# Graph attention on one core: edge terms in three bf16 parts, and the attributes' share of the logits from 49 TensorE products

## The reference

```python
edge_emb = edge_attr_full @ ew.T + eb
xw = x @ W
xj = xw[src].reshape(-1, H, D) + edge_emb.reshape(-1, H, D)
xi = xw[dst].reshape(-1, H, D)
alpha = leaky_relu(einsum(xi, att_i) + einsum(xj, att_j))     # a logit per edge and head
amax = segment_max(alpha, dst); ea = exp(alpha - amax[dst])
alpha = ea / (segment_sum(ea, dst)[dst] + EPS)
aggr = segment_sum(xj * alpha[..., None], dst)
return aggr.mean(axis=1) + b
```

## Time and profile before

| | |
|---|---|
| median of 3 runs | 3387.27 us (3385.08 to 3389.48) |
| span of the profiled execution, which is its own time here | 3764.7 us |
| PE busy | 2439.0 us, 65% |
| DVE busy | 2004.0 us, 53% |
| POOL busy | 2210.5 us, 59% |
| ACT busy | 696.7 us, 19% |
| DMA, mean of the 16 engines | 195.78 MB, 52 GB/s over the span |
| first gather of layer 0 | at 475.50 us |

### The profile page before, as it was taken

The page is one execution under the profiler, slowest core; times in us unless marked ns, Lnnn a source line. Parts: engine busy times, 40 slices in busy tenths (PEclk is TensorE's granted clock), DMA queues, the critical chain, the costliest instruction groups (busy, mean ns, idle before and its releaser), DMA issues.

```text
span 3764.7 us, 48376 instructions
## 1 busy us (share of the span) xinstructions
PE 2439.0 (65%) x13595; PEld 2001.4 (53%) x13595; DVE 2004.0 (53%) x6216; ACT 696.7 (19%) x3102; POOL 2210.5 (59%) x2357
## 2 busy tenths in 40 slices
PE   6779726666582766658276665837576582766668
PEld 6679615555461655547165554725455461655546
DVE  8955624554472555547255554725454472555456
ACT  0078511111121111112111111211111121111112
POOL 0067466666626766662666666266676626666661
PEclk8555555555565555556555555655555565555556
DMA  3212122222202222221222222022222202222221
GB/s 101 97 60 80 30 52 54 53 52 57 49 24 51 54 51 53 56 49 30 47 54 52 53 56 49 25 53 54 50 53 57 50 24 50 54 50 53 52 49 40
DMA packets 114121, 195.78 MB, mean 52 GB/s; under 512 B 39897, under 2 KB 77272, under 8 KB 113864
## 3 DMA queue, kind: packets, MB, share of 16 engines
q0 software_dynamic: 62560, 130.25, 15.2%
q1 hardware_dynamic: 51304, 62.42, 5.3%
HBM read 180.86 MB, written 11.67 MB: 51 GB/s over the span
## 4 chain that ended last, share of the span: by engine, by line
DVE 36%; PE 25%; another core or an unknown queue 20%; issue 13%; DVEq 3%; POOL 1%; ACT 1%; ACTq 1%; DMA 0%; POOLq 0%
PE bank L745 10%; PE bank L747 6%; DVE acc L1200 4%; DVE into L1143 2%; DVEq L1016 2%; PE bank L718 2%; DVE pw L1161 2%; DVE alpha L1094 2%; PE bank L741 2%; PE bank L783 2%; DVE fwd L1150 2%; DVE lanes L1129 2%; DVE prod L1072 1%; PE bank L766 1%
## 5 line engine op out<-in xcount | busy, mean ns | idle before, releaser
L510 POOL DMA_INDIRECT ring<-table,srci x1955 | 1941.2, 993 | 937.6 <-issue 556.4
L745 PE MATMUL bank<-pw,ring 128*128 128x48 f32 x3910 | 1210.9, 404 | 203.3 <-issue 201.8
L745 PEld LDWEIGHTS bank<-pw,ring 128*128 128x128 f32 x3910 | 1014.9, 314 | 302.9 <-issue 231.1
L1200 DVE TENSOR_TENSOR acc<-acc,bank 128x288 f32 x490 | 222.8, 455 | 1128.7 <-remote 857.3
L747 PE MATMUL bank<-onehot,est 128*36 128x24 f32 x3910 | 632.6, 243 | 222.9 <-issue 221.7
L741 PE MATMUL bank<-zeros 128*128 128x288 bf16 x490 | 208.5, 426 | 697.1 <-DVE pw L1161 438.7
L747 PEld LDWEIGHTS bank<-onehot,est 128*36 128x36 f32 x3910 | 391.2, 149 | 393.9 <-issue 226.6
L741 PEld LDWEIGHTS bank<-zeros 128*128 128x128 bf16 x490 | 55.4, 113 | 752.0 <-DVE pw L1161 453.3
L586 ACT ACTIVATE dd<-dd 128x66 f32<-128x66 f32 x75 | 19.4, 258 | 2163.4 <-DVE dd L1154 1177.9
L580 ACT COPY ai_win<-ai_rows 128x48 f32 x1955 | 336.3, 229 | 432.6 <-issue 410.5
L491 POOL TENSOR_TENSOR ring<-ring,acc 128x512 f32<-128x512 f32 x98 | 117.1, 1195 | 250.1 <-ACT ring L545 246.7
(11 more groups left out here) (214 smaller groups left out, 2610.1 us busy)
## 6 DMA issues: line engine op xcount, KB each, us to landing
ring<-table,srci POOLq DMA_INDIRECT x1955
ai_rows<-lo_dram SPq DMA_DIRECT2D x28, 896.0 KB, 4.3
at<-in_attr SPq DMA_DIRECT2D x65, 224.0 KB
table<-ring SPq DMA_DIRECT2D x15, 390.0 KB, 3.5
table<-ring SPq DMA_DIRECT2D x5, 325.0 KB, 3.4
result<-ring SPq DMA_DIRECT2D x24, 64.0 KB
x_mid<-ring SPq DMA_DIRECT2D x3, 384.0 KB, 2.7
table<-ring SPq DMA_DIRECT2D x5, 130.0 KB, 2.4
```

What stands on the lines that cost most here:

```text
L510: nc.gpsimd.indirect_dma_start(out=ring[:, slot(t), :], out_offset=None, in_=table, in_offset=bass.IndirectOffsetOnAxis(ap=srci[:, t:t + 1 ...
L745: nc.tensor.matmul(wide[:, 0:H, at_k], ring[:, slot(t), 0:D], pw[:, g % DEEP, k, :, :], start=False, stop=False, skip_group_check=True)
L1200: V.tensor_tensor(win, win, grp_sum(g).rearrange("p (r w) -> p r w", r=REG), ALU.add)\
```

## The change

1. **Edge terms in three parts.** est gets a last axis of three f32 numbers (12 bytes a column). The first is the value as before. Two subtractions at the end of chain_probs (DVE) make the second, the value less its upper half read as bf16, and the third, the second less its own upper half. PE's edge product no longer reads the f32 values but the upper two bytes of all three parts (`est_high`), 108 columns of bf16, one product with a bf16 `onehot`. The host repeats every row of the edge weights and biases three times, so that the later product with `El` adds the parts up; for the maxima and the sums a new reduction (node_sums) adds them, and the masks of phi_mask take their new rows. est_ready is now raised by the second subtraction, and PE waits for it ahead of the edge products of a chunk's first group.
2. **The order on PE.** The four ring products of a group come first, then its four edge products.
3. **The attributes' share once.** The host gives the attributes a second time, turned (`attr_turned`, 3.2 MB, loaded into parts of est and S). PE makes the share of all edges, for all five layers and both heads, in 49 products (eight tiles each, 80 columns from `vblock`), two behind each of the 25 output products ahead of layer 0. ACT takes them from the banks with nine copies into `e_stage`, SP stores it (`e_dram`, 2.0 MB), and SP loads a chunk's share (`et`) beside its attributes. L1087 and L1093 go, and L1096 adds `et`. POOL's gathers of layer 0 wait for the store (e_w).
4. **onehot** is bf16. In the graph convolution, where PE needs it in f32, each piece is made in one of two f32 buffers and copied to `onehot`.

```diff
-        onehot = sb("onehot", [P, TILES, WIN])
+        onehot = sb("onehot", [P, TILES, WIN], BF16)
-        est = sb("est", [P, 2, K, EC])
+        est = sb("est", [P, 2, K, EC, NP3])
+        et = sb("et", [P, NAT, K, H])
+        estf = est[:, :, :, :, :].rearrange("p b k e q -> p (b k e q)")
+        est_high = estf.bitcast(BF16).rearrange("p (b k e two) -> p b k e two", b=2, k=K, two=2)[:, :, :, :, 1]
+        first_part, second_part, third_part = (est[:, :, :, :, q] for q in range(NP3))
+        first_high, second_high = (est_high.rearrange("p b k (e q) -> p b k e q", q=NP3)[:, :, :, :, q] for q in range(2))
...
+            def e_chunk(gc):
+                layer, c = divmod(gc, NC)
+                a = layer * TILES * H
+                sp.dma_start(et[:, gc % NAT, 0:CH[c], :].rearrange("p k h -> p (k h)"),
+                             e_dram[:, a + TC[c] * H:a + TC[c + 1] * H]).then_inc(e_in[gc % NAT], 16)
...
+            sp.dma_start(turned[0], attr_turned[:, 0:E_CUT * P]).then_inc(turned_in, 16)
+            sp.dma_start(turned[1], attr_turned[:, E_CUT * P:NBLK * P]).then_inc(turned_in, 16)
...
+            sp.wait_ge(e_out, NFILL)
+            sp.dma_start(e_dram, e_stage.rearrange("p l t h -> p (l t h)")).then_inc(e_w, 16)
...
                         sp.wait_ge(est_ready, gc + 1)
                         attr_chunk(gc + NAT)
+                        e_chunk(gc + NAT)
...
+                if layer == 0:
+                    pool.wait_ge(e_w, 16)
...
+            act.wait_ge(gcn_sums, GCN_G)
+            for q in range(NFILL):
+                a, b = q * FILL * BLK, min(TILES, (q + 1) * FILL * BLK)
+                act.wait_ge(e_ps, q + 1)
+                nc.scalar.copy(e_stage[:, :, a:b, :].rearrange("p l t h -> p t l h"),
+                               bank[E_BANKS[q % len(E_BANKS)]][:, 0:(b - a) * LH]
+                               .rearrange("p (t l h) -> p t l h", l=LAYERS, h=H)).then_inc(e_out, 1)
...
-                    ins = nc.tensor.matmul(total[:, at_k], rows[:, g % 3, k, :], onehot[:, t0 + k, :],
+                    ins = nc.tensor.matmul(total[:, at_k], rows[:, g % 3, k, :], gcn_hot[c % 2][:, i * GRP + k, :],
...
+            def edge_products(first, last):
+                for b in range(first, last):
+                    q, i = divmod(b, FILL)
+                    if i == 0 and q >= len(E_BANKS):
+                        pe.wait_ge(e_out, q - len(E_BANKS) + 1)
+                    part, at_b = (turned[0], b) if b < E_CUT else (turned[1], b - E_CUT)
+                    ins = nc.tensor.matmul(bank[E_BANKS[q % len(E_BANKS)]][:, i * BLK * LH:(i + 1) * BLK * LH],
+                                           part[:, at_b * P:(at_b + 1) * P],
+                                           vblock[:, :, :].rearrange("p b q -> p (b q)"), start=True, stop=True)
+                    if i == FILL - 1 or b == NBLK - 1:
+                        ins.then_inc(e_ps, 1)
...
+                edge_products(2 * j, min(NBLK, 2 * j + 2))
+            pe.wait_ge(e_out, NFILL)
...
+                for k in range(n):
+                    nc.tensor.matmul(wide[:, 0:H, spots[k]], ring[:, slot(t0 + k), 0:D], pw[:, g % DEEP, k, :, :],
+                                     start=False, stop=False, skip_group_check=True)
+                if t0 == TC[c]:
+                    pe.wait_ge(est_ready, layer * NC + c + 1)
                 for k in range(n):
                     t = t0 + k
-                    nc.tensor.matmul(wide[:, 0:H, at_k], ring[:, slot(t), 0:D], pw[:, g % DEEP, k, :, :],
-                                     start=False, stop=False, skip_group_check=True)
-                    ins = nc.tensor.matmul(wide[0:EC, H, at_k], est[:, c % 2, t - TC[c], :], onehot[:, t, :],
+                    ins = nc.tensor.matmul(wide[0:EP, H, spots[k]], est_high[:, c % 2, t - TC[c], :], onehot[:, t, :],
                                            start=False, stop=k == n - 1, skip_group_check=True)
...
-                V.tensor_tensor(onehot[:, cs, :], r_e[:, cs].unsqueeze(2).broadcast_to((P, K, WIN)),
+                V.tensor_tensor(gcn_hot[c % 2], r_e[:, cs].unsqueeze(2).broadcast_to((P, K, WIN)),
                                 iota_f.unsqueeze(1).broadcast_to((P, K, WIN)), ALU.is_equal).then_inc(onehot_done, 1)
+                v.wait_ge(onehot_done, c + 1)
+                V.tensor_copy(onehot[:, cs, :], gcn_hot[c % 2])
...
                 if part == 0:
-                    v.wait_ge(at_in[gc % NAT], 16 * (gc // NAT + 1))
-                    link(V.tensor_tensor(pr, at[:, gc % NAT, 0:k, :].unsqueeze(1).broadcast_to((P, H, k, FA)),
-                                         v17[:, layer, :, 0:FA].unsqueeze(2).broadcast_to((P, H, k, FA)), ALU.mult))
-                if part == 1:
                     v.wait_ge(win_ready, gc + 1)
                     link(V.tensor_tensor(win, win, onehot[:, ts, :].unsqueeze(2).broadcast_to((P, k, H, WIN)), ALU.mult))
-                if part == 2:
-                    V.tensor_reduce(ee[:, 0:hk], prod[:, 0:hk * FA].rearrange("p (q f) -> p q f", f=FA), AX, ALU.add)
+                if part == 1:
                     link(V.tensor_reduce(alpha[:, :, 0:k].rearrange("p h k -> p k h"), win, AX, ALU.add))
                     v.sem_inc(win_used, 1)
+                    v.wait_ge(e_in[gc % NAT], 16 * (gc // NAT + 1))
                     link(V.tensor_tensor(alpha[:, :, 0:k], alpha[:, :, 0:k],
-                                         ee[:, 0:hk].rearrange("p (h k) -> p h k", h=H), ALU.add))
+                                         et[:, gc % NAT, 0:k, :].rearrange("p k h -> p h k"), ALU.add))
...
-                V.tensor_tensor(es[:, :, 0:HF].rearrange("p k (h f) -> p k h f", h=H),
-                                at[:, gc % NAT, 0:k, :].unsqueeze(2).broadcast_to((P, k, H, FA)),
-                                pr.unsqueeze(3).broadcast_to((P, k, H, FA)), ALU.mult).then_inc(est_ready, 1)
+                whole = mark(V.tensor_tensor(es[:, :, 0:HF].rearrange("p k (h f) -> p k h f", h=H),
+                                             at[:, gc % NAT, 0:k, :].unsqueeze(2).broadcast_to((P, k, H, FA)),
+                                             pr.unsqueeze(3).broadcast_to((P, k, H, FA)), ALU.mult))
                 v.wait_ge(step, done)
                 for g in GC[c][0:2 if c else AHEAD]:
                     weigh(layer, g)
+                v.wait_ge(step, whole)
+                rest, last = second_part[:, c % 2, 0:k, :], third_part[:, c % 2, 0:k, :]
+                link(V.tensor_tensor(rest, es, first_high[:, c % 2, 0:k, :], ALU.subtract))
+                V.tensor_tensor(last, rest, second_high[:, c % 2, 0:k, :], ALU.subtract).then_inc(est_ready, 1)
...
-                for part in range(3):
+                for part in range(2):
                     windows_sum(layer, 0, part)
...
+                link(V.tensor_reduce(ns, nsT[:, :, 0:2 * H * NP3].rearrange("p j (q r) -> p q j r", r=NP3), AX, ALU.add))
```

More of the change, by code:

```diff
@@ L31 @@
 EC = HF + 2 * H
+NP3 = 3
+BLK = P // FA
+NBLK = TILES // BLK
+LH = LAYERS * H
+FILL = 6
+NFILL = -(-NBLK // FILL)
+E_BANKS = (0, 1, 2, 3, 6, 7)
+E_CUT = 33
+EP = EC * NP3
+SPC = HF * NP3
 BIG = 1e30
@@ L164, in program @@
         sc = sb("sc", [P, 4, H, NT])
+        node_sums = sb("node_sums", [P, 2 * H, NT])
         y = sb("y", [P, 2, D])
@@ L290, in program @@
         att_ps = sem("att_ps")
+        turned_in = sem("turned_in")
+        e_ps = sem("e_ps")
+        e_out = sem("e_out")
+        e_w = sem("e_w")
+        e_in = [sem(f"e_in{i}") for i in range(NAT)]
         cnt_max = sem("cnt_max")
@@ L442, in _ @@
                 table_tiles(layer)
+                if layer == 0:
+                    sp.wait_ge(e_w, 16)
+                    for gc in range(NAT):
+                        e_chunk(gc)
                 for c in range(NC):
@@ L1233, in _ @@
                     for i, g in enumerate(GC[c]):
-                        if more and scan_at >= 2 and i < 3:
+                        if more and scan_at >= 2 and i < 2:
                             windows_sum(layer, c + 1, i)
@@ L1257, in _ @@
                         v.wait_ge(lay_e, 32 * (layer + 1))
-                        V.tensor_tensor(El[0:EC, :], El[0:EC, :], Bl, ALU.add).then_inc(El_sum, 1)
+                        V.tensor_tensor(El[0:EP, :], El[0:EP, :], Bl, ALU.add).then_inc(El_sum, 1)
                 unlink()
```

63 lines of the change are left out of this document (44 added, 19 removed).

## The result

The changed kernel takes 3413.5 us (median of 4 runs, 3409.2 to 3414.2), the kernel before, beside it, 3387.8 us. The ratio is 1.0074, with a 95% interval of 1.0060 to 1.0088: slower by 25.6 us, where 15.7 was forecast. The profiled execution of the changed kernel shows no sign of a recording cost: it spans 3412.1 us.

The account below looks back on a forecast made before the run. POOL's gathers at 1.25 us, not PE, were taken to bound the edge stages. From 3387.3 us, +50 for holds, -39 for the tail and +5 before the layers gave 3403 us; range 3345 to 3460.

Parts of the forecast that it names:

- The bound: Edge stage of each layer: POOL's 391 gathers at 1.25 us (489 us) set the time; PE's groups need only 335.
- Rival C: Edge stages: late completions are real and gathers wait for PE, so much faster, 2830 to 3300 us; chance 0.13.
- The late completions are a cost of recording: PE's late completions in the profile: recording adds 377 us, 75 per layer, and eases with six pieces a tile, not eight.
- The tail: After a layer's last gather: 28.3 us, shortened by 8.3, or 7.8 net of the added reduction; 39 us in five layers.
- The holds: Gathers waiting for long two-input DVE instructions: 23.1 us a layer before; the change adds 10 a layer, 50 in all.
- Subtractions at 12 bytes: Two added DVE subtractions in chain_probs: reading with a 12-byte step gives 1.35 ns an element, 1.5 us each.
- Rival E: Edge stages: two-input operations no longer hold anything, holds unchanged by the edit, 3353 us; chance 0.05.
- B: Subtractions run at the contiguous rate and hold fewer gathers, 20 us (6 to 34): faster, 3373 us; chance 0.22.
- D: Subtractions pay the full price of a step, 91 us of holds: slower, 3455 us; chance 0.12.
- F: PE's edge products: strided bf16 weights load no faster than f32, group 3.4 us, tail gains almost nothing: 3439 us; chance 0.10.
- Before the layers: Added products, store, masks and casts ahead of layer 0: mostly hidden, +5 us, from +3 to +12.
- node_sums: Added DVE reduction over 300 elements, on the tail's path: 0.44 us.

Follow-up runs that it names:

- order_only: Kernel before, only with the four ring products of a group ahead of its four f32 edge products: 3341.0 us (0.9866).
- tail_alternates: Kernel before with the order of order_only in chunks 0 to 11 and the old alternation in chunks 12 to 14: 3373.6 us (0.9955).
- no_subs: Changed kernel without the two subtractions at the end of chain_probs (edge terms wrong): 3342.0 us (0.9873).
- share_back: Changed kernel with the attributes' product and its reduction put back into windows_sum, result unused: 3419.7 us (1.0095).
- contig_reads: Changed kernel with both subtractions reading contiguous numbers, still writing 12 bytes apart (edge terms wrong): 3413.2 us (1.0064).
- split: Changed kernel with L1174, L1259, L1267 and L1268 each in four back-to-back pieces in chunks 0 to 11: 3350.9 us (0.9894).
- split_linked: As split, with DVE waiting for each piece before it starts the next: 3308.6 us (0.9769).
- late_third: Changed kernel with its second subtraction (L1268) moved behind the next group's addition for chunks 1 to 12: 3505.7 us (1.0341).
- pieces7: Kernel before with the order of order_only and L1087, L1091, L1175 in seven pieces with waits, chunks 0 to 11: 3261.8 us (0.9618).

## Why the prediction was right

The forecast, 3403, was 10 us short of 3413.5, inside the range, with the right sign. The mechanism was the one forecast: two more long operations hold gathers, and a shorter tail gives part of it back. That the holds came out at nearly the number is in part luck, as said below. Its steps:

- **The bound.** Gathers at 1.25 us, not PE, set a stage. Right: PE got 1.3 us a group faster and the stages longer. Rival C (hundreds of us) is out, by the result and by order_only, whose gathers stay at 996 ns.
- **The late completions are a cost of recording.** Mostly right, with a rest. order_only records as many instructions and takes no longer recorded than not, and the time it loses unrecorded is 46 us, not 377. But its cause is not the number of pieces, as the sum said ("six pieces a tile instead of eight"): it is the alternation with f32 weights of 36 columns. The span fell below the forecast 3450 to 3700 for that reason. And 13.7 us of real time that alternating costs lie in the stages of before, which the working had in its 23.1 us of holds.
- **The tail.** Before: 28.3 forecast, 30.2 as tail_alternates shows it. After: 20.5 forecast (28.3 less 7.8), 24.2 measured, both means of five layers. The gain was to be 39 us and was (30.2 - 24.2) x 5 = 30. This is the term that was mis-sized. PE was even faster than assumed (2.13 us a group for 2.35), so DVE alone sets that stretch: from the last part of the chunk's gathers (L1188 at 1554.30) to the first group's addition of chunk 13 it is 38.3 us for the 34.4 in the sum. The sum ran DVE's chain as if additions, weights and the wait of each addition for the step before it (0.55 us "DVE fwd", "DVE maxes") took nothing from it. no_subs shows how much of the tail the two subtractions are: 3.1 us a layer (21.1 for 24.2), where the sum had 2 for the wait for the parts (T + 15.5 for the 13.85 of 11.5 and one group, and the 0.3).

```profile
1554.30 0.27 DVE L1188 TENSOR_TENSOR alpha<-alpha,ring 128x56 f32<-128x56 f32 x1 [13.62 <-DMA ring<-table,srci]
...
1579.73 0.45 DVE L1288 TENSOR_TENSOR acc<-acc,bank 128x288 f32 x1 [0.56 <-DVE fwd L1206]
1585.88 1.04 DVE L1288 TENSOR_TENSOR acc<-acc,bank 128x288 f32 x2 [0.55 <-DVE maxes L1239]
...
1592.57 0.46 DVE L1288 TENSOR_TENSOR acc<-acc,bank 128x288 f32 x1 [0.56 <-DVE acc L1279]
```

- **The holds.** 50 forecast. By the sum's own reckoning, the period of before, 582.4, leaves 582.4 - 488.7 - 30.2 - 41.6 = 21.9 us a layer above gathers, tail and the stretch between; the changed kernel has 32.5 (the mean of its five stages, 521.2, less 488.7): 53 us more in five layers. The number is right, but it has two parts of which the sum had one. The gathers themselves are held by 64 us more, 162 against the 98 of order_only (70 against the recorded 92 of before), and the 13.7 us that alternating had cost in the stages are gone. Together that is 50, near the 53. The sum had put the 13.7 down to holds and had too few new ones (50 for 64); that the two cancel is luck. In the changed kernel the two subtractions hold 71 us; L1259 holds 44.5 us where L1175 held 34 (before) or 32 (order_only), with its output 12 bytes apart, where the text had writing apart at "nearly none"; and L1087's leaving freed nothing in the stages (share_back: 1026 ns with it, 1029 without), since what follows it moves into its place.
- **Subtractions at 12 bytes.** The size was right, the reason not. Forecast were 1.35 ns an element and 1.5 us; in a chunk of 28 tiles they take 1.54 and 1.52 us in the timeline above, 1.36 ns an element over the fixed 0.15. The 1435 and 1422 ns of the groups by line are means that take in the chunks of 16 and 11 tiles. The prediction read such means as those of full chunks too: its 0.97 ns an element side by side is (1.08 - 0.15) by 896 = 1.04 for L1175. And it let the reading set the rate, while contig_reads shows that the writing does. The Trainium skill, "Advanced Engine Details and Errata", section "SBUF Cachelines", asks for at least two accesses on each 16-byte line. The prediction read it as speaking for a rate between, and the trace agrees: 1.36 ns lies between the 1.04 side by side and the 1.7 of L1143 at 16 bytes.
- **Two-input operations hold gathers.** Rival E is out. no_subs, split, split_linked and late_third moved the unrecorded time by -71, -63, -105 and +92 us; the holds in their traces moved by -57 (with 15 in the tail), -68, -105 and +96. The sentence of the Trainium skill, "SBUF — State Buffer", section "Who interferes with whom", that `tensor_tensor` did not stall DMAs issued from GpSimd doesn't hold for these indirect DMAs.
- **B and D** differed in what the subtractions hold. B wanted them at 1.35 us or less and the second to meet nothing; they took 1.52, and the second held a gather in all 65 places. They hold 51 and 20 us in the trace, and leaving them out gives 57 back: between the 6 to 34 of B and the 91 of D. D's 91 doesn't follow from the working's own rate: (2 x 1.86 - 1.03) x 13 x 5 x 0.47 is 82.
- **F** is out: an edge pass is 0.09 us, forecast 0.1.
- **Before the layers.** +5 forecast, 3.6 measured (479.08 against 475.50). The 49 products fit, and the steps even got shorter, 1.28 us.
- **node_sums**, forecast 0.44, is 0.468 us.

Put together: stages +53, tail -30, before the layers +3.6, between the layers (41.9 against 41.6, by 5) +1.5, in all +28 against the measured +25.6.

What stays open: where the 13.7 us lie that alternating costs in the stages of before; why alternating with f32 weights of 36 columns makes completions late in a recorded execution; and when a held gather is let in between two operations without a pause (at 1305.67 in the trace after it was, in split it was passed over three times).

## What to carry to other kernels

Where one engine issues DMAs at a steady beat and its beat is the bound, look at what lengthens single beats, not at the busiest engine: long two-input operations on DVE did here, and cutting them into pieces with a wait between gave 2.4% (order_only to pieces7) and 3.1% (the changed kernel to split_linked) without touching the arithmetic. Work that is added to an engine with time to spare isn't free if it holds such a beat, and work that is taken from it may give nothing back, because what follows moves into its place. A group's mean over mixed shapes is not the time of its main shape (1.42 against 1.52 us here). And two kinds of matmul that alternate can cost more than the same ones in two runs: exchanging two loops was worth 46 us, while the whole rewrite around it cost 72.

## What the hardware showed beyond that

- Alternating f32 weights of 128 and 36 columns cost 0.84 us a tile (3.42 a group) where the same products in two runs cost 2.53 a group. With bf16 weights of 108 columns beside the same f32 ones it cost nothing (2.14 against 2.13).
- That same alternation made the recorded execution 377 us longer than the unrecorded ones. No other kernel here, some with more instructions, showed a difference above 0.3%; so a span that stands far from the median is to be explained before its waits are read.
- A held gather is let in at the end of the holding operation when DVE then waits; in a run of two-input operations without a pause it was passed over up to three ends (2.51 us for 0.94). A gather that asks in the last 0.1 us or so of an operation isn't held (105 gathers at L1179 in split).
- Reductions and additions from PSUM held nothing: in the changed kernel 65 gathers ask during the reduction L1176 and 73 during the additions L1288 (one input from SBUF, one from PSUM), and none takes over 0.95 us.
- Writing f32 12 bytes apart cost DVE 1.36 ns an element for the 1.04 side by side; reading 12 bytes apart as well added nothing.
